# The widest probability tile of each head normalised by GpSimd instead of VectorE

## The reference, cut to what matters

```
x = layernorm(x + attention0(x))      # 16 heads of 64, keys and values from a latent of 64, causal
x = layernorm(x + experts(x))         # 16 experts, top 2, and a shared one
x = layernorm(x + attention1(x))      # 16 heads of 16, causal
x = layernorm(x + spikes(x))          # 1024 wide, squared relu, 5 spiking steps
```

```
s = q @ k.T / 8                        # 512 x 512, causal mask
p = exp(s - max(s)) / sum(exp(s - max(s)))
y = p @ v
```

## Time and profile before

| what | value |
|---|---|
| median of 3 runs | 1912.42 us (1912.19 to 1920.85) |
| profiled execution, its time | 1911.52 us |
| its span | 1909.8 us |
| TensorE busy | 1687.9 us, 88% |
| VectorE busy | 1218.6 us, 64% |
| ScalarE busy | 1005.5 us, 53% |
| GpSimd busy | 572.5 us, 30% |
| mean granted TensorE clock | 0.946 |

### The profile page before, as it was taken

How to read it: one execution, slowest core, us unless ns; L and a number is a source line. 1 busy time by engine, 2 the same in 40 slices (tenths; PEclk the granted TensorE clock), 3 DMA queues, 4 the chain that set the end, 5 groups by cost and what they waited for, 6 DMA issues and landing times. The chain is left out here.

```text
span 1909.8 us, 33114 instructions
## 1 busy us (share of the span) xinstructions
PE 1687.9 (88%) x9186; PEld 1172.0 (61%) x9187; DVE 1218.6 (64%) x4191; ACT 1005.5 (53%) x2496; POOL 572.5 (30%) x713
## 2 busy tenths in 40 slices
PE   6899999999999999987879986799999998599997
PEld 4666666656666665757557764566666664356675
DVE  1886868687777868662764435588888777313445
ACT  1774757475665747552223335366667766554431
POOL 2001010000101010100374438788998773200001
PEclk9999999999999999996779998699999999899999
DMA  4211111021111111102024442888887767010000
GB/s 115 50 40 40 39 36 42 17 61 22 50 33 44 33 44 39 44 12 88 1 79 136 136 99 75 146 133 141 139 140 134 123 120 94 2 43 17 22 18 33
DMA packets 82736, 128.04 MB, mean 67 GB/s; under 512 B 14752, under 2 KB 40832, under 8 KB 82480
## 3 DMA queue, kind: packets, MB, share of 16 engines
q1 hardware_dynamic: 71216, 100.11, 25.6%
q0 software_dynamic: 9664, 25.94, 5.8%
q10 hardware_dynamic: 1728, 0.55, 0.2%
HBM read 73.60 MB, written 35.65 MB: 57 GB/s over the span
## 5 line engine op out<-in xcount | busy, mean ns | idle before, releaser
L136 ACT ACTIVATE c_probs<-c_probs,a_negmax 128x128 f32<-128x128 f32 (+3 forms) x512 | 279.6, 550 | 0.0
L1730 ACT ACTIVATE c_probs<-a_ps_st 128x384 f32<-128x384 f32 (+1 forms) x384 | 189.7, 526 | 124.9 <-PE a_ps_st L1555 122.1
L126 DVE CUSTOM_DVE_ANT_0 c_probs<-a_ps_score,c_mask 128x128 f32<-128x128 f32 (+3 forms) x512 | 221.2, 487 | 35.3 <-PE a_ps_score L432 17.9
L174 ACT ACTIVATE c_probs<-a_ps_trans 128x512 f32<-128x512 f32 (+1 forms) x256 | 124.7, 487 | 225.0 <-PE a_ps_trans L162 224.1
L1860 DVE CUSTOM_DVE_ANT_0 a_junk<-a_ps_score,c_mask 128x128 f32<-128x128 f32 (+3 forms) x512 | 220.5, 486 | 28.1 <-PE a_ps_score L1533 23.6
L615 POOL TENSOR_SCALAR a_rstd<-a_mv 128x4 f32<-128x4 f32 x8 | 1.8, 228 | 784.8 <-DVE a_mv L607 784.8
L162 PE MATMUL a_ps_trans<-c_ident,c_probs 128*128 128x128 f32 x1280 | 195.2, 285 | 40.1 <-DVE c_probs L146 26.2
L162 PEld LDWEIGHTS a_ps_trans<-c_ident,c_probs 128*128 128x128 f32 x1280 | 149.6, 144 | 113.2 <-issue 51.3
L431 PE MATMUL a_ps_score<-a_kh,a_qs 128*128 128x128 f32 (+3 forms) x512 | 169.2, 354 | 24.3 <-DVE a_negmax L126 16.5
L1391 POOL TENSOR_TENSOR a_ms<-a_ms,c_minus_half 128x16 f32<-128x16 f32 x64 | 187.3, 2929 | 2.2 <-DVE a_ms L1829 2.2
L1555 PE MATMUL a_ps_st<-a_qs,a_ks 128*128 128x512 f32 (+3 forms) x512 | 152.1, 360 | 16.9 <-ACT c_probs L1730 8.8
(11 more groups left out here) (228 smaller groups left out, 3191.7 us busy)
## 6 DMA issues: line engine op xcount, KB each, us to landing
a_qs<-a_qlow SPq DMA_DIRECT2D x128, 128.0 KB, 2.2
bounce<-a_words SPq DMA_DIRECT2D x64, 256.0 KB, 2.1
a_qs<-bounce SPq DMA_DIRECT2D x128, 128.0 KB, 5.1
a_ks<-bounce SPq DMA_DIRECT2D x128, 128.0 KB, 5.7
slot_out<-m_y SPq DMA_DIRECT2D x80, 128.0 KB, 1.7
a_xT<-in_xT SPq DMA_DIRECT2D x8, 512.0 KB, 3.6
a_xtok<-in_x SPq DMA_DIRECT2D x8, 512.0 KB, 4.7
token_rows<-c_X SPq DMA_DIRECT2D x8, 512.0 KB, 5.7
```

Of the source, the lines that this page charges most:

```text
L126: dve.tensor_tensor_reduce(out=self.prob[:, h % 4, QOFF[i]:QOFF[i] + keys], in0=self.ps_score[g][:, at:at + keys], in1=self.C.mask[:, L - ...
L136: act.activation(at, at, ACT.Exp, scale=-1.0, bias=self.negmax[:, h % 4, i:i + 1], accum_out=self.rowsum[:, h % self.ring, i:i + 1]).then_ ...
L1730: act.activation(probT[:, r8, col:col + width], ps_st[item % 2][:, 0:width], ACT.Exp).then_inc(s_stc, 1)
```

## The change

`normalise` on VectorE stops after the three narrower tiles. A new step, `normalise_widest`, runs on GpSimd: it waits for the head's reciprocal, multiplies the 128x512 tile in place and counts on a semaphore of its own, `s_norm_wide`. The first group of transposes waits for three counts per head of `s_norm` and for one of `s_norm_wide`. GpSimd's queue has, per batch, the weight loads and then the 16 tiles; the root of the batch before stands behind head 3, and that of the last batch at the end.

```diff
@@ class Softmax, __init__
+        self.s_norm_wide = S.sem("norm_wide")
@@ normalise
-        for i in range(TT):
+        for i in range(TT - 1):
             at = self.prob[:, h % 4, QOFF[i]:QOFF[i + 1]]
             dve.tensor_scalar(at, at, self.recip[:, r, i:i + 1], None, ALU.mult
                               ).then_inc(self.s_norm, 1)
 
+    def normalise_widest(self, pool, n, h):
+        pool.wait_ge(self.s_recip, n + 1)
+        i, r = TT - 1, h % self.ring
+        at = self.prob[:, h % 4, QOFF[i]:QOFF[i + 1]]
+        pool.tensor_scalar(at, at, self.recip[:, r, i:i + 1], None, ALU.mult).then_inc(self.s_norm_wide, 1)
+
@@ transposes
             if g == 0:
-                pe.wait_ge(self.s_norm if self.normed else self.s_exp, n * TT + TT)
+                pe.wait_ge(self.s_norm, n * (TT - 1) + TT - 1)
+                pe.wait_ge(self.s_norm_wide, n + 1)
@@ layer0_attention, GpSimd's queue
                 for b in range(B):
                     meanwhile(pool, b)
-                    ln.root(pool, b)
+                    for h in range(H):
+                        sm.normalise_widest(pool, b * H + h, h)
+                        if h == 3 and b >= 1:
+                            ln.root(pool, b - 1)
+                ln.root(pool, B - 1)
```

## The result

The changed kernel takes 1935.74 us (1933.89 to 1938.78, 4 runs) against 1913.68 us (1912.19 to 1920.85, 4 runs) of the kernel before on the same chip: a ratio of 1.0109, with a 95% interval of 1.008 to 1.0139. It is slower by 22 us; forecast was 1928, slower by 16. The profiled execution of it took 1938.78 us.

What follows compares the result with a forecast made beforehand. TensorE was taken to set the pace in the first attention, with about 70 us idle. 1911.5 + 16.4 - 1.3 = 1926.6, plus 0.9 for the median, gave 1927.5, say 1928 us; range 1902 to 1966.

Steps and rivals of the forecast that it cites:

- The bound: First attention: TensorE sets the pace, about 70 us idle; 26.2 us of it are 35 waits of transposes for the normalisation.
- VectorE's 0.39 per head: Normalisation on VectorE: losing the 512-column multiplication saves 0.39 us per head; the three that stay last 0.88 us.
- D = 1.0: Duration of GpSimd's 128x512 multiplication per head: taken as 1.0 us, with 0.61 and 1.81 as the ends.
- Exclusion for D - 0.14: VectorE's SBUF multiplications and GpSimd's tile exclude each other for all but 0.14 us of GpSimd's duration.
- The blocked row: Routing stage: a 64-column VectorE tensor_scalar takes 1.27 us instead of 0.20 beside a GpSimd tensor_tensor of 1.26.
- Ready D - 0.53 later: All four normalised tiles ready later than before by GpSimd's duration less 0.53 us: 0.47 us later.
- 35 heads: Heads whose transposes wait for the normalisation: 35, each delayed by 0.47 us, 16.4 us in all.
- The moved loads, -1.3 us: GpSimd's weight DMAs no longer run beside a normalisation: 0.18 us in each of 7 batches, 1.3 us returned.
- The second wait, the root, head 0 behind the loads: nothing: TensorE's added wait (at most 6 us), the root's new place and head 0's tile behind the weight loads counted as 0.
- Full overlap: Rival: ports don't exclude each other in this stage, tiles ready 0.27 us earlier; -16 us, 1896; chance 0.14.
- Line rate: Rival: exclusion holds but GpSimd's tile takes 0.61 to 0.72 us; 1914 to 1918 us; chance 0.24.
- Slow GpSimd: Rival: GpSimd's tile takes 1.3 to 1.81 us, tiles 0.77 to 1.28 later; 1938 to 1978 us; chance 0.18.

Runs made afterwards that it cites:

- experiment 2: Changed kernel with the widest tile's multiplication left out: VectorE multiplies three tiles, GpSimd none; ratio 0.9904 to the kernel before, 18.5 us less.
- experiment 6: Changed kernel with GpSimd's tile started only when VectorE's three are done; ratio 1.0299 to the kernel before, 58 us more.
- experiment 1: Changed kernel with VectorE multiplying all four tiles, GpSimd's new queue order and TensorE's second wait kept; ratio 0.9998 to the kernel before.
- experiment 5: Kernel before, GpSimd's queue in the new order, plus an unread GpSimd multiplication of 128 to 512 columns after VectorE's four tiles; ratio 0.9958.
- experiment 7: Changed kernel with VectorE's reciprocal moved ahead of the next head's masked maxima; 1902.59 us against 1925.86 of the kernel before, ratio 0.9874.
- experiment 4: Kernel before, GpSimd's queue in the new order, plus an unread 128x512 GpSimd multiplication per head beside VectorE's four tiles; ratio 1.0233.
- experiment 9: Kernel before with only GpSimd's queue changed: weight loads wait for head 15's reciprocal, the root for a reciprocal too; ratio 0.9969, 6 us less.

## Why the prediction was right, and which of its steps were not

*The bound.* Right: the wait of the transposes in every second head sets the price. Experiments 2 and 6 move it down by 0.39 and up by 1.2 us and the time follows, by -18.5 and +58 us.

*VectorE's 0.39 per head.* Right as a duration (0.88 for three tiles, experiments 1 and 2), and gone again in the changed kernel.

*D = 1.0.* Wrong: 1.57 by itself, 1.72 in place. The choice between a fixed surplus and one by the column went to the wrong side; L807's 0.606 at 128 columns is the 0.610 of experiment 5, so that its being a comparison did not matter, and the surplus over the copy grows with the columns: 1.57 is near the 1.81 of that reading and not near the 0.91 of the fixed one. The Trainium skill's rule of roughly line rate for one-input operations (GPSIMD Engine Reference, section 4.1 Engine selection) holds for the copy's 0.609 and not for this operation with a scalar per partition, which takes 2.6 times as long.

*Exclusion for D - 0.14.* Wrong: 0.43 in the changed kernel, 0.77 in two stretches where VectorE has a fourth tile. The blocked row was one short VectorE instruction that began at the start of a GpSimd instruction with two inputs, and I took its length for the rule; why that one was held up for 1.1 us and these for 0.43 no run shows. The Trainium skill's exclusive lock for the whole instruction (SBUF — State Buffer, Who interferes with whom) does not agree with the third tile, which takes 407 ns inside GpSimd's instruction and 414 without it. The same section says that a VectorE instruction with at most one input in SBUF, outside the 2-port modes, does not contend with GpSimd; that agrees, with 686 ns for the widest maximum beside GpSimd (experiment 7) and 686 in the kernel before.

*Ready D - 0.53 later.* The two errors cancel: 1.0 + 0.74 = 1.74 us after the group's start was forecast, 1.78 measured, later by 0.50 instead of 0.47. The number was right for a wrong reason. With the true D and the step as it stood, the sum would have been 1.04 x 35 = 36 us; with the true exclusion and D = 1.0, there would have been next to no loss.

*35 heads.* Short: 49 waits now, head 4 of the batches among them, at 0.50 each 24.5 us; measured are 26.0 more in the transposes and 4.7 less in the scores. A wait of 0.34 grows to 0.90, by 0.56, since TensorE starts 0.10 after the last tile instead of 0.05.

*The moved loads, -1.3 us.* Mis-sized: -6 us (3 to 9 by the interval). I counted the stretched normalisation and not VectorE's gap behind it, which stands in the earlier trace rows as "issue 14.9" and was not used; it accounts for half.

*The second wait, the root, head 0 behind the loads: nothing.* Right within the noise; the 0.05 us above, if it is the second wait's, would be 2.5 us in 49 waits, which experiment 1 can't exclude. In head 0 GpSimd starts 0.98 after the group and ends at 2.74, and TensorE's weight load for the transposes comes 1.28 us later still.

*The rivals.* Full overlap, which was meant beside VectorE's own tiles, did not come about; in experiment 7 GpSimd overlaps fully, but with the maxima. Line rate is refuted by D. Slow GpSimd had the right D (1.57 lies in its 1.3 to 1.81) and the wrong price, since 1.25 of GpSimd's 1.72 us are spent beside VectorE's three tiles.

## What to carry to other kernels

An instruction moved to a slower engine costs its full length from the moment that its input is ready, so the input has to be made early: here 1.57 us on GpSimd cost 22 us behind the old reciprocal and gain 24 us behind an early one, both with the 6 us of the moved loads in them. Before two engines are put side by side, ask which instructions of the other run in that stretch, and put GpSimd's SBUF work beside VectorE's reads of PSUM. When a forecast rests on a product of two unknowns, measure each by itself: a right sum does not show that its terms are.

## What the runs showed that was not expected

- GpSimd's tensor_scalar with a scalar per partition takes 0.61, 0.93, 1.25 and 1.57 us for 128 to 512 columns, its copy of 512 columns 0.609.
- One GpSimd instruction of 512 columns holds up VectorE's SBUF to SBUF multiplications twice, for 0.43 and 0.34 us, and lets one through in between.
- A delay in VectorE's queue is dearer than one of GpSimd's tile alone: 0.77 us in VectorE's queue (experiment 4) cost 45 us, 58 for each us of delay; on GpSimd 1.2 us (experiment 6) cost 58 and 0.50 us (the change) 22, 48 and 44 for each.
- A wait of TensorE can shrink without any gain, when the products ahead of it run at a granted clock of 0.50 instead of 0.96 (experiment 9).
- Weight loads that nobody in the stage waits for cost 6 us by their place (experiment 9).
